# A mixture-of-experts layer whose first six batches are sorted by expert through a table in HBM, and the last two left dense

## The chip, the cores and the metric

The kernel runs on one core of one Trainium2 chip, as one launch. The metric is the device time of the launch in microseconds (us); before the change the median of three runs is 338.32 us (337.97 to 338.34). One core has five engines that run their own instruction streams in order and meet at semaphores: PE (matmuls; its weight loads are listed as PEld), DVE (vector), ACT (activations), POOL (GpSimd, which also issues the indirect DMAs) and SP, which only issues DMAs here.

## The reference, cut to what matters

```
h = embeddings[x]                              # 8 batches of 256 tokens, width 256
h = h + attention(layernorm(h))                # 16 heads of 16, rotary q and k, softmax
n = layernorm(h)
chosen = argmax(n @ gate_w.T)                  # one of 8 experts for each token
h = h + n + (n @ expert_w[chosen].T)
```

Everything is fp32. The kernel multiplies with float32r operands that are split into a high and a low part, so each product is three matmuls for each of the two halves of the contraction: high by high, low by high, high by low.

## The kernel before, in words

The kernel is a software pipeline over the eight batches, each of two tiles of 128 tokens (`NT = 2`). `steps` runs a step `b` from -3 to 9; each step has 16 slots, and in each slot every engine's program holds the pieces whose table entry falls on it. In step `b` stand, side by side: the attention of batch `b` (`visit`, eight visits in the even slots: scores of batch `b+1` for the row maxima, and transposed scores of batch `b` for `exp`; `outputs` in slots 5, 9, 13 and 1 of the next step), the front of batches `b+2` and `b+3` (layernorm, q/k/v projection, rotary sum on POOL, transposes; tables `FRONT` and `EARLY`), the part after attention of batch `b` or `b-1` (`POST`, and `LAST` for batch 7: output projection, residual, layernorm, gate, `choose`), and the experts of batch `b-2`. The step of the last attention is step 7; steps 8 and 9 hold what is left of batches 6 and 7.

`restack` (SP, L284 and L279) copies the split q and k of batch `b+2` into `stacks`, ten DMAs of 128 or 256 KB, and it starts when DVE has written the last low part (`qk_low`, front slot 4, slot 2 for the first four batches). `maximum` (SP, L269) brings the row maxima into the same buffer. `stacks` has three buffers.

The experts are dense: all 8 experts are computed for all tokens. `experts` on PE is called eight times for a batch, and each such unit is one token tile by two experts, 6 matmuls of 128x512 (`product`, L419). `select` on DVE (L881, L885) adds each expert's 128x256 result times a 0/1 mask. `finish` on POOL (L363) adds the two accumulators into `res`, and SP stores it (`store`, L289). `unit_in` says in which slots the units lie. The units of batches 0 to 4 share one PSUM bank, those of 5 to 7 use four.

Of the kernel before, what the change touches and what calls it, by code (L numbers as in the profile page):

```python
# [15 lines left out]
P = 128  # L16
# [5 lines left out]
VALS = 3  # L22


def rope_tables(n, hd):
# [7 lines left out]
    return np.ascontiguousarray(both.reshape(n // P, P, 2, hd).transpose(1, 0, 2, 3))  # L33


def tower(nc, x, emb, w_qkv, w_proj, gate_w, expert_w, rope, ramp, out):
# [12 lines left out]
    with ExitStack() as ctx:  # L49
# [11 lines left out]
        ramp_sb = sb("ramp_sb", [P, N_EXP])  # L61
# [20 lines left out]
        x_l = sb("x_l", [P, C, NT, P], F32R)  # L82
        rope_a = sb("rope_a", [P, NT, 2 * NH, HD])
# [9 lines left out]
        vals = [sb(f"vals{i}", [P, NT, NH, STRIP]) for i in range(VALS)]  # L93
        neg_max = sb("neg_max", [P, 2, NT, 8])
# [17 lines left out]
        yn = sb("yn", [P, NT, D])  # L112
        y_h = [sb(f"y_h{i}", [P, C, NT, P], F32R) for i in range(2)]
        y_l = [sb(f"y_l{i}", [P, C, NT, P], F32R) for i in range(2)]
        base = sb("base", [P, NT, D])
# [6 lines left out]
        res = sb("res", [P, NT, D])  # L122
# [37 lines left out]
        exp_ps, acc_ok, res_ok, out_ok = map(sem, "expert_ps acc_ok res_ok out_ok".split())  # L160

# [64 lines left out]
        def expert_banks(b):  # L226
# [23 lines left out]
        def _(sp):  # L250
# [5 lines left out]
            sp.dma_start(ramp_sb[:, :], ramp).then_inc(rope_in, 16)  # L256
# [29 lines left out]

            def store(b):
                wait(sp, res_ok, b + 2)
                sp.dma_start(out[b].rearrange("(t p) d -> p t d", p=P), res[:, :, :]).then_inc(out_ok, 16)  # L289

            def step(b, p):
# [9 lines left out]
                if here(b, -2):  # L301
# [12 lines left out]
            sp.wait_ge(out_ok, 16 * (NB + 1))  # L314
# [3 lines left out]
        def _(pool):  # L318
# [6 lines left out]
                            pattern=[[-1, P]], channel_multiplier=1).then_inc(ident_ok, 1)  # L325
            pool.wait_ge(ids_in, 16)

# [28 lines left out]
            def residuals(b):  # L356
                wait(pool, g_normed, b * NT + NT)
                g.tensor_tensor(base[:, :, :], h1[:, :, :], yn[:, :, :], ALU.add).then_inc(base_ok, 1)

            def finish(b):  # L360
                wait(pool, acc_ok, b * 16 + 17)
                wait(pool, out_ok, b * 16 + 16)
# [14 lines left out]
            def step(b, p):  # L377
                for s in range(SLOTS):
# [10 lines left out]
                    if s == 0 and here(b, -3):  # L389
                        finish(b - 3)  # L390
                    if s == 6 and b == -2:
# [18 lines left out]
        def _(pe):  # L410
# [156 lines left out]
            def y_transpose(b):  # L567
                wait(pe, g_normed, b * NT + NT)
                for c in range(C):
                    for t in range(NT):  # L570
                        k = (c * NT + t) * P
                        m = tr(m_bank[:, k:k + P], yn[:, t, c * P:(c + 1) * P], ident[:, :])
# [19 lines left out]
            def experts(b, p, n, banks):  # L592

# [395 lines left out]
```

## Time and the profile before

| | us |
|---|---|
| median of three runs | 338.32 (337.97 to 338.34) |
| the profiled execution | 337.72 |
| its span (first to last instruction) | 335.9 |
| PE busy / DVE busy / ACT busy / POOL busy | 280.2 / 244.5 / 118.4 / 84.7 |
| 16 DMA engines, share of the span on SP's queue | 38.6% |

The span is what the profile's rows lie in; the profiled execution's own time is 1.8 us longer, and it is 0.6 us under the median. PE's busy time is modelled, since matmuls overlap: a unit of six matmuls shows six records of about 0.40 us that start 0.23 us apart, so the pitch and not the length is the cost. PEclk is the granted TensorE clock, 1.00 for 2.4 GHz and 0.50 for 1.2 GHz.

### The profile page before, as it was taken

Reading aid. Unit: us, or ns where it says so; the run is one execution under the profiler, and the core shown is the slowest. Engines: PE = TensorE matmul, PEld = TensorE weight load, DVE = VectorE, ACT = ScalarE, POOL = GpSimd, SP = SyncE. Lnnn points to the kernel's source line nnn. Section 1 sums busy time; section 2 is a strip of 40 time slices with the busy share of each in tenths; the row PEclk is TensorE's granted clock in tenths of the full one; section 3 lists DMA queues with packets and bytes.
Section 4 is the critical chain, followed back from the end, with each engine's and each line's share of the span. In section 5 each row is a group of like instructions: output and inputs, shape, how many; then the busy total and the mean of one; then the engine's idle time right before and its main releaser. Section 6 shows DMA issues by size and latency. Waiting matters only on the chain.

```text
span 335.9 us, 5461 instructions
## 1 busy us (share of the span) xinstructions
PE 280.2 (83%) x2000; PEld 200.0 (60%) x2000; DVE 244.5 (73%) x595; ACT 118.4 (35%) x245; POOL 84.7 (25%) x96
## 2 busy tenths in 40 slices
PE   0457281877698899999999899989999999999894
PEld 0345170555465577766776677667766766667673
DVE  8353254678769887988798879887988885657763
ACT  3012131246354544434443444344434453441000
POOL 5235248472201310222032303220210121120211
PEclk9995755589979999999999999999999999999999
DMA  3619699009809608800790079008900000000000
GB/s 112 254 45 129 71 104 104 0 11 119 83 3 125 68 0 101 92 4 31 99 93 5 31 101 93 2 31 101 94 28 8 0 4 33 2 1 33 0 31 31
DMA packets 16197, 19.13 MB, mean 57 GB/s; under 512 B 2524, under 2 KB 13607, under 8 KB 16044
## 3 DMA queue, kind: packets, MB, share of 16 engines
q1 hardware_dynamic: 15404, 18.25, 38.6%
q0 software_dynamic: 768, 0.55, 1.3%
q8 instruction: 16, 0.26, 0.4%
q14 instruction: 9, 0.07, 0.1%
HBM read 5.30 MB, written 2.10 MB: 22 GB/s over the span
## 4 chain that ended last, share of the span: by engine, by line
PE 41%; DVE 23%; issue 11%; POOL 9%; DMA 7%; SPq 4%; ACT 3%; POOLq 0%; DVEq 0%; ACTq 0%
PE e_bank L419 13%; PE f_bank L419 7%; PE o_bank L536 6%; DVE acc L885 5%; DVE neg_max L806 4%; POOL qk L345 3%; PE t_pair L501 3%; DMA stacks<-parts 3%; DMA stacks<-max_rows 3%; SPq L284 3%; PE s_pair L419 2%; POOL h L332 2%; PE m_bank L548 2%; PE m_bank L419 2%; POOL res L363 1%
## 5 line engine op out<-in xcount | busy, mean ns | idle before, releaser
L687 ACT ACTIVATE probs<-t_pair 128x512 f32<-128x512 f32 x128 | 69.7, 597 | 91.4 <-PE t_pair L501 90.9
L806 DVE TENSOR_REDUCE neg_max<-s_pair 128x2 f32<-128x512 f32 x120 | 76.7, 681 | 14.0 <-PE s_pair L473 14.0
L419 PE MATMUL e_bank<-ew_h,y_h 128*128 128x512 f32 x92 | 40.4, 439 | 4.6 <-DVE acc L881 2.7
L501 PE MATMUL t_pair<-stacks 50*128 50x256 f32 x192 | 35.1, 310 | 3.9 <-DMA stacks<-max_rows 1.9
L885 DVE SCALAR_TENSOR_TENSOR acc<-e_bank,mask,acc 128x256 f32<-128x256 f32 x66 | 28.8, 477 | 11.3 <-PE e_bank L419 10.9
L501 PEld LDWEIGHTS t_pair<-stacks 50*128 50x128 f32 x192 | 24.4, 186 | 20.7 <-issue 17.1
L419 PE MATMUL e_bank<-ew_h,y_l 128*128 128x512 f32 x92 | 36.3, 395 | 0.0
L419 PE MATMUL e_bank<-ew_l,y_h 128*128 128x512 f32 x92 | 36.3, 395 | 0.0
L536 PE MATMUL o_bank<-probs,vals 128*32 128x256 f32 x512 | 35.1, 393 | 1.3 <-ACT max_rows L662 1.3
L473 PE MATMUL s_pair<-stacks 48*128 48x256 f32 x176 | 35.1, 325 | 0.4 <-DVE neg_max L806 0.4
L345 POOL TENSOR_TENSOR qk<-rope_a,rope_b 128x512 f32<-128x512 f32 x16 | 20.7, 1292 | 54.8 <-DVE rope_b L793 54.8
L419 PE MATMUL f_bank<-wqkv_h,x_h 128*128 128x256 f32 (+1 forms) x56 | 22.8, 407 | 10.8 <-DVE parts L798 6.5
L473 PEld LDWEIGHTS s_pair<-stacks 48*128 48x128 f32 x176 | 24.6, 197 | 1.5 <-DVE neg_max L806 0.6
L419 PEld LDWEIGHTS e_bank<-ew_h,y_h 128*128 128x128 f32 x92 | 17.3, 188 | 12.1 <-DVE acc L885 3.9
L429 PE MATMUL f_bank<-ident,xn 128*128 128x128 f32 x32 | 6.4, 333 | 19.5 <-DVE xn L774 18.8
L536 PEld LDWEIGHTS o_bank<-probs,vals 128*32 128x32 f32 x512 | 13.7, 110 | 14.1 <-issue 6.2
L419 PE MATMUL f_bank<-wqkv_l,x_h 128*128 128x256 f32 (+1 forms) x56 | 21.3, 380 | 0.0
L419 PE MATMUL f_bank<-wqkv_h,x_l 128*128 128x256 f32 (+1 forms) x56 | 21.2, 379 | 0.0
L419 PEld LDWEIGHTS f_bank<-wqkv_h,x_h 128*128 128x128 f32 x56 | 12.5, 222 | 14.2 <-DVE parts L798 7.3
L419 PEld LDWEIGHTS e_bank<-ew_l,y_h 128*128 128x128 f32 x92 | 17.3, 188 | 4.2
L352 POOL TENSOR_SCALAR g_ve<-g_mv 128x2 f32<-128x2 f32 x8 | 2.0, 252 | 69.8 <-DVE g_mv L765 69.8
L419 PEld LDWEIGHTS e_bank<-ew_h,y_l 128*128 128x128 f32 x92 | 17.4, 189 | 2.1
(123 smaller groups left out, 557.0 us busy)
## 6 DMA issues: line engine op xcount, KB each, us to landing
stacks<-parts SPq DMA_DIRECT2D x48, 128.0 KB
stacks<-parts SPq DMA_DIRECT2D x12, 256.0 KB
ew_raw<-in_expert_w SPq DMA_DIRECT2D x1, 2048.0 KB, 7.9
late_stacks<-parts SPq DMA_DIRECT2D x16, 128.0 KB
out<-res SPq DMA_DIRECT2D x8, 256.0 KB, 2.1
late_stacks<-parts SPq DMA_DIRECT2D x4, 256.0 KB
probs<-in_w_qkv SPq DMA_DIRECT2D x2, 384.0 KB, 3.4
stacks<-max_rows SPq DMA_DIRECT2D x24, 8.0 KB
```

Source lines behind the costliest of these rows:

```text
L284: sp.dma_start(stacks[b % STACKS][at:at + HD, :, k, :].bitcast(F32), parts[:, half, part, :].bitcast(F32)).then_inc(stack_in, 16)
L332: g.indirect_dma_start(h0[:, j, :], None, emb, bass.IndirectOffsetOnAxis(ap=ids[:, j:j + 1], axis=0), bounds_check=V - 1, oob_is_err=False ...
L345: g.tensor_tensor(qk[:, t, :, :, :].rearrange("p g d j -> p g j d"), rope_a[:, t, :, :].rearrange("p (g j) d -> p g j d", j=8), rope_b[:, ...
L419: m = mm(o, a(c), w(c), start=(n == 0), stop=(n == 3 * C - 1))
L429: m = tr(f_bank[:, k:k + P], xn[:, t, c * P:(c + 1) * P], ident[:, :])
L473: m = mm(score_pair(b, v)[:, half, t * N:(t + 1) * N], stacks[b % STACKS][r:r + KS, pair, 0, t * P:(t + 1) * P], stacks[b % STACKS][r:r + ...
L501: m = mm(t_pair[:, half, c * N:(c + 1) * N], stacks[b % STACKS][r:r + KM, pair, 1, c * P:(c + 1) * P], stacks[b % STACKS][r:r + KM, pair, ...
L536: m = mm(o_bank[STRIP * j:STRIP * (j + 1), 0:N], vals[b % VALS][:, c, head(4 * g + j), :], probs[:, (4 * g + j) % RING, c, :], start=(c == ...
L548: m = tr(strips_bank(b, t)[:, g * P:(g + 1) * P], o_t[:, g, t * P:(t + 1) * P], ident[:, :])
L687: nc.scalar.activation(probs[:, (2 * v + half) % RING, :, :].rearrange("p c n -> p (c n)"), t_pair[:, half, :], ACT.Exp, scale=SCALE).then ...
L806: v.tensor_reduce(neg_max[:, k // 4, :, 4 * half + k % 4], score_pair(b, k)[:, half, :].rearrange("p (t n) -> p t n", t=NT), AX.X, ALU.max ...
L885: v.scalar_tensor_tensor(out=acc[:, j, t, :], in0=y, scalar=mask[:, p, t, e:e + 1], in1=base[:, t, :] if u == 0 else acc[:, j, t, :], op0= ...
```

## The change

Batches 0 to 5 (`ROUTED = 6`) have no dense experts any more. For each of them PE counts with five small matmuls (`count_places`) how many tokens of each expert stand before each token, DVE turns that into a row number in a table in HBM (`find_rows`), in which each expert has its own region, and POOL scatters the layernormed rows with their residual base and their token number (2064 bytes for each token) into `sorted_rows` with two indirect DMAs (`send_rows`). This happens in slot 2 of step `b+2`. After batch 5, in step 7, DVE computes from the counts which expert and which first row each of 19 blocks of 128 rows has (`plan_blocks`, 17 small operations), and POOL writes 128 blank rows behind each expert's last one (`send_blanks`, 8 indirect DMAs). There are always 19 blocks, 12 + 7, whatever the tokens choose. They are taken in ten pairs (the last holds one block): SP fetches a pair (`fetch`, each block's row number read into a register), PE transposes it (`turn_blocks`), ACT and DVE split it (`block_top`, `block_rest`), PE multiplies each block by its one expert (`block_products`, 12 matmuls of 128x256 for a pair, the expert's column read into a register), DVE adds the base (`block_result`) and POOL scatters the rows to the output (`send_results`, an indirect DMA for each block). Pair `m` is turned in slot 11 + `m` counted from the start of step 7 and multiplied in the slot after. The buffers of fetched pairs are three. Batches 6 and 7 stay dense; batch 6's units move to slots 6 to 13 of step 8, behind the last pair, and batch 7's to the even slots of step 9, all with four banks.

`base` and `yn` get two buffers, with waits for the scatter two batches back. The small input `ramp` grows to a table of 284 columns. Two constant matrices are made on POOL at the start.

```diff
-            return [e_bank, f_bank] + s_bank if b >= NB - 3 else [e_bank]
+        expert_banks = [e_bank, f_bank] + s_bank
+        turn_bank = [f_bank, e_bank]
+        def place_at(b):
+            return SLOTS * (b + 2) + 2
+        def turn_at(m):
+            return SLOTS * (NB - 1) + 11 + m
...
-            slots = (0, 1, 2, 3, 5, 7, 8, 10) if b == NB else (1, 3, 5, 7, 9, 11, 13, 14) if b == NB - 1 else tuple(range(0, NH, 2))
+            slots = tuple(range(6, 14)) if b == NB else tuple(range(0, NH, 2))
...
+            def fetch(m):
+                if m == 0:
+                    sp.wait_ge(plan_ok, PLAN)
+                    sp.wait_ge(blanks_out, 16 * N_EXP)
+                    for i in range(2):
+                        sp.wait_ge(rows_out[i], 16 * NT * ROUTED // 2)
+                if m >= 3:
+                    sp.wait_ge(routed_out[(m - 3) % 2], sent(m - 3))
+                for j in blocks_of(m):
+                    row = sp.value_load(block_row[0:1, j:j + 1], min_val=0, max_val=N_EXP * REGION - P)
+                    sp.dma_start(fetched[m % 3][j % 2], sorted_rows[bass.ds(row, P), :]).then_inc(block_in[m % 3], 16)
...
+            def send_rows(b):
+                wait(pool, row_at_ok, b + 1)
+                wait(pool, row_ids_ok, b + 1)
+                wait(pool, base_ok, b + 1)
+                for t in range(NT):
+                    g.indirect_dma_start(sorted_rows, bass.IndirectOffsetOnAxis(ap=row_at[:, b, t:t + 1], axis=0),
+                                         rows[b % 2][:, t, :], None, bounds_check=N_EXP * REGION - 1,
+                                         oob_is_err=False).then_inc(rows_out[b % 2], 16)
+            def send_blanks():
+                g.memset(blank[:, 0:2 * D], 0.0).then_inc(blank_ok, 1)
...
+                for e in range(N_EXP):
+                    g.indirect_dma_start(sorted_rows, bass.IndirectOffsetOnAxis(ap=blank_at[:, e:e + 1], axis=0),
+                                         blank[:, :], None, bounds_check=N_EXP * REGION - 1,
+                                         oob_is_err=False).then_inc(blanks_out, 16)
+            def send_results(m):
+                wait(pool, block_ok, m + 1)
...
+                                         result[m % 2][:, j % 2, :], None, bounds_check=NB * N - 1,
...
-            def experts(b, p, n, banks):
+            def experts(b, p, n):
+                if k == 0 and n == 0:
+                    wait(pe, block_ok, PAIRS)
...
+            def count_places(b):
+                wait(pe, mask_ok, b * NT + NT)
+                mm(e_bank[:, 0:N_EXP], upper[:, :], mask[:, p, 0, :], start=True, stop=True)
...
+            def turn_blocks(m):
+                wait(pe, block_in[m % 3], fetches(m))
+                wait(pe, bl_ok, m - 1)
...
+                for j in blocks_of(m):
+                    for c in range(C):
+                        k = (j % 2 * C + c) * P
+                        i = tr(turn_bank[m % 2][:, k:k + P], fetched[m % 3][j % 2][:, c * P:(c + 1) * P], ident[:, :])
+                i.then_inc(bt_ps, 1)
+            def block_products(m):
...
+                wait(pe, bl_ok, m + 1)
+                wait(pe, block_ok, m - 1)
+                for j in blocks_of(m):
+                    w = pe.value_load(block_column[0:1, j:j + 1], min_val=0, max_val=(N_EXP - 1) * D)
+                    i = product(s_bank[m % 2][:, j % 2 * D:(j % 2 + 1) * D],
...
+                i.then_inc(block_ps, 1)
...
+                    for m in range(PAIRS):
+                        if g_at == turn_at(m):
+                            turn_blocks(m)
+                        if g_at == turn_at(m) + 1:
+                            block_products(m)
...
+            def block_top(m):
+                wait(act, bt_ps, m + 1)
...
+            def find_rows(b):
+                wait(dve, place_ps, b + 1)
...
+                            find_rows(k)
+                            if k == ROUTED - 1:
+                                plan_blocks()
```

## Rows read from the trace of the kernel before

**Rows 1.** The page's busy time by engine: busy us, share of the span, instructions.
```profile
PE 280.2 (83%) x2000; PEld 200.0 (60%) x2000; DVE 244.5 (73%) x595; ACT 118.4 (35%) x245; POOL 84.7 (25%) x96
```
**Rows 2.** Busy time by stretch, cut where an attention step begins; last three columns PEclk, DMA share, GB/s.
```profile
91.80:118.20 26.40, 23.13 (x202) 15.82 (x202) 21.83 (x55) 13.55 (x29) 5.56 (x7) 0.94 0.56 62
118.20:151.30 33.10, 32.29 (x252) 23.49 (x250) 27.96 (x69) 13.67 (x29) 5.83 (x7) 1.00 0.44 50
...
218.20:248.00 29.80, 28.66 (x235) 20.72 (x233) 23.96 (x55) 13.34 (x28) 4.73 (x5) 1.00 0.53 64
248.00:275.70 27.70, 26.77 (x216) 18.59 (x216) 23.36 (x59) 11.86 (x25) 3.50 (x4) 1.00 0.04 12
275.70:302.00 26.30, 26.06 (x187) 17.41 (x188) 15.09 (x48) 11.24 (x24) 3.90 (x5) 1.00 0.03 12
302.00:335.90 33.90, 27.58 (x142) 20.46 (x140) 20.82 (x60) 1.96 (x4) 5.63 (x6) 0.99 0.07 24
```
**Rows 3.** The chain that ended last, single pieces: start us, us, what.
```profile
42.48 2.94 PE f_bank L419 x12
...
59.77 1.10 PE f_bank L429 x4
...
195.59 1.44 PE f_bank L419 x12
...
299.20 1.40 PE s_pair L419 x6
...
302.42 1.00 PE o_bank L536 x16
303.42 1.60 PE f_bank L419 x6
...
306.42 0.44 PE m_bank L548 x4
...
314.51 0.07 issue
```
**Rows 4.** Groups of instructions over the whole run: count, busy us, mean ns, idle before.
```profile
L885 DVE SCALAR_TENSOR_TENSOR acc<-e_bank,mask,acc 128x256 f32<-128x256 f32 x66 | 28.8, 477 | 11.3 <-PE e_bank L419 10.9
...
L851 DVE TENSOR_TENSOR y_l<-m_bank,y_h 128x512 fp32r<-128x512 f32 x8 | 5.4, 679 | 1.2 <-ACT y_h L662 1.2
L662 ACT ACTIVATE y_h<-m_bank 128x512 fp32r<-128x512 f32 x8 | 4.7, 590 | 7.0 <-PE m_bank L572 6.9
...
L859 DVE TENSOR_REDUCE score<-m_bank 128x16 f32<-128x32 f32 x8 | 1.5, 182 | 1.3 <-PE m_bank L588 1.3
...
L321 POOL MEMSET ident<- 128x128 f32 x1 | 0.2, 205 | 0.4 <-POOLq L982 0.4
```
**Rows 5.** Timeline of SP's queue in the first step without experts: start us, us.
```profile
99.89 0.59 SPq L279 DMA_DIRECT2D stacks<-parts  x1
...
107.46 19.33 SPq L269 DMA_DIRECT2D late_stacks<-max_rows  x4
```
**Rows 6.** One microsecond at that restack's end, columns as in rows 2.
```profile
114.00:115.00 1.00, 1.00 (x20) 0.59 (x12) 0.90 (x2) 0.00 (x0) 0.02 (x1) 1.00 0.33 35
```
**Rows 7.** Timeline of POOL: the second gather of batch 0.
```profile
4.91 1.00 POOL L332 DMA_INDIRECT h<-in_emb,ids  x1 [0.30 <-DVE h L949]
```
**Rows 8.** Timeline of DVE: its first instruction that reads that gather.
```profile
7.38 0.42 DVE L762 BATCH_NORM_STATS2 f_st<-h 128x6 f32<-128x256 f32 x1
```
**Rows 9.** DMA issues of the run: size, median us from issue to landing.
```profile
out<-res SPq DMA_DIRECT2D x8, 256.0 KB, 2.1
...
probs<-in_w_proj SPq DMA_DIRECT2D x1, 256.0 KB, 2.8
```
**Rows 10.** Tile `h`, all 16 gathers: from issue to landing.
```profile
DMA to landing us min/median/max: 5.2/7.8/10.9
```
**Rows 11.** Two stretches of four microseconds, columns as in rows 2.
```profile
62.00:66.00 4.00, 3.73 (x11) 2.56 (x12) 2.18 (x5) 1.04 (x3) 2.52 (x2) 0.55 0.00 0
66.00:70.00 4.00, 2.89 (x18) 1.88 (x17) 3.96 (x7) 1.46 (x3) 2.30 (x2) 1.00 0.00 0
```

More of the change, by code:

```diff
@@ L82, in tower, with over @@
         x_l = sb("x_l", [P, C, NT, P], F32R)
+        ROW = 2 * D + 4
+        with ExitStack() as late:
+            def over(name, shape, dt=F32):
+                return late.enter_context(nc.sbuf_tensor(name, shape, dt))
+            blank = over("blank", [P, ROW])
+            blank_at = over("blank_at", [P, N_EXP], U32)
+            n_rows = over("n_rows", [P, N_EXP])
+            fuller = over("fuller", [P, N_EXP, ROUTED * NT])
+            n_blocks = over("n_blocks", [P, N_EXP])
+            lower = over("lower", [P, N_EXP, N_EXP])
+            block_end = over("block_end", [P, N_EXP])
+            block_start = over("block_start", [P, N_EXP])
+            begun = over("begun", [P, BLOCKS, N_EXP])
+            ended = over("ended", [P, BLOCKS, N_EXP])
+            owner = over("owner", [P, BLOCKS, N_EXP])
+            shift = over("shift", [P, N_EXP])
+            first_row = over("first_row", [P, BLOCKS, N_EXP])
+            owned_row = over("owned_row", [P, BLOCKS, N_EXP])
+            row_sum = over("row_sum", [P, BLOCKS])
+            column_sum = over("column_sum", [P, BLOCKS])
+            block_row = over("block_row", [P, BLOCKS], I32)
+            owned_column = over("owned_column", [P, BLOCKS, N_EXP])
+            block_column = over("block_column", [P, BLOCKS], I32)
+            result = [over(f"result{i}", [P, 2, D]) for i in range(2)]
+            res = over("res", [P, NT, D])
         rope_a = sb("rope_a", [P, NT, 2 * NH, HD])
@@ L300, in step @@
                     maximum(b + 1, 0)
-                if here(b, -2):
+                if b == NB - 1:
+                    for m in range(PAIRS):
+                        fetch(m)
+                if here(b, -2) and not routed(b - 2):
                     store(b - 2)
@@ L325, in _, with upper_triangle @@
                             pattern=[[-1, P]], channel_multiplier=1).then_inc(ident_ok, 1)
+            g.memset(upper[:, :], 1.0).then_inc(pool_filled, 1)
+            g.memset(every[:, :], 1.0).then_inc(every_ok, 1)
             pool.wait_ge(ids_in, 16)
+            def upper_triangle():
+                pool.wait_ge(pool_filled, 3)
+                g.affine_select(out=upper[:, :], in_=upper[:, :], compare_op=ALU.is_ge, fill=0.0, base=0,
+                                pattern=[[1, P]], channel_multiplier=-1).then_inc(upper_ok, 1)
@@ L642, in step @@
                         outputs(b, (s - 5) // 4)
-                    if here(b, -2) and unit_in(b, s) is not None:
-                        experts(b - 2, p, unit_in(b, s), expert_banks(b - 2))
+                    for k in range(ROUTED):
+                        if g_at == place_at(k):
+                            count_places(k)
+                    for m in range(PAIRS):
+                        if g_at == turn_at(m):
+                            turn_blocks(m)
+                        if g_at == turn_at(m) + 1:
+                            block_products(m)
+                    if here(b, -2) and not routed(b - 2) and unit_in(b, s) is not None:
+                        experts(b - 2, p, unit_in(b, s))
                     for k in batches(post, "o0", g_at):
@@ new lines, in block_rest, with block_result @@
+            def block_rest(m):
+                n = len(blocks_of(m)) * D
+                wait(dve, bh_ok, m + 1)
+                wait(dve, block_ps, m - 1)
+                v.tensor_tensor(block_low[m % 2][:, 0:n], turn_bank[m % 2][:, 0:n], block_high[m % 2][:, 0:n].bitcast(F32),
+                                ALU.subtract).then_inc(bl_ok, 1)
+            def block_result(m):
+                n = len(blocks_of(m))
+                wait(dve, block_ps, m + 1)
+                if m >= 2:
+                    wait(dve, routed_out[m % 2], sent(m - 2))
+                both = wide_raw[:, 2 * (m % 3) * ROW:2 * (m % 3 + 1) * ROW].rearrange("p (j r) -> p j r", j=2)
+                v.tensor_tensor(result[m % 2][:, 0:n, :], s_bank[m % 2][:, 0:n * D].rearrange("p (j d) -> p j d", d=D),
+                                both[:, 0:n, D:2 * D], ALU.add).then_inc(block_ok, 1)
```

218 lines of the change are left out of this document (189 added, 29 removed).

## The prediction

> **What bounds the kernel now.** I read the busy times by engine first [rows 1]: PE is at 83%, DVE at 73%, but these are averages. So next the stretches, cut where an attention step begins [rows 2]. The reader is to see three regimes. The stretch from 91.8 has no experts yet and lasts 26.4 us. The three from 118.2 to 218.2 have a batch of dense experts each and last 100.0 us together, with PE busy 32.3 of 33.1: PE bounds them. From 218.2 the fronts run out (29.8, 27.7, 26.3), PE still full. The last 33.9 us are experts of batches 6 and 7 and the end. Then the chain that ended last [rows 3] gives what pieces of PE cost at each clock, and SP's and POOL's timelines and the DMA rows [rows 5 to 10] what the transfers cost.
>
> **What goes away.** A dense unit costs PE 1.40 us in the chain [rows 3], a batch of eight 11.2 us. DVE loses 16 selects of 0.477 us, 7.6 us [rows 4].
>
> **Steps 2 to 4 (118.2 to 218.2).** The floor by PE is 33.3 - 11.2 = 22.1 us. But the stretch from 91.8 is nearly what such a step becomes: the same attention, front and gate work, no experts, 26.4 us, PEclk 0.94 [rows 2]. Its slow clock at the start costs about 1.5 us; against that the new step adds five small matmuls (0.5), five small DVE operations of about 0.18 us plus hops (1.2, [rows 4]), and on POOL two scatters, which there nothing waits for. That makes 25 to 26. The other limit is the restack. In that stretch SP issued it at 99.89, 8.1 us in [rows 5], and the DMA engines were busy until about 115 [rows 6], so 15 us, and the scores that open the next step wait for it. The later fronts hand over two slots later, about as late as 8 to 9 us in, which gives 23.5 to 24.5 us, and the scatter of 528 KB lands on the same engines just then, up to 2 us more. I take 25.8 us for each step, because both limits end there; bounds 24 (no interference) and 28 (the scatter adds whole, the clock falls). Three steps: 77.4 instead of 100.0.
>
> **Step 5 (29.8).** PE's part would be 18.6, but batch 7's restack still runs: 24.5, bounds 23 and 27. **Step 6 (27.7).** No restack left; PE 16.5, DVE 23.4 - 7.6 + 1.2 = 17.0: with their waits on one another 19, bounds 17.5 and 21. Saved so far: 22.6 + 5.3 + 8.7 = 36.6 us, and step 7 begins at 239.1 instead of 275.7 (bounds 231 and 250). Everything ahead of 118.2 stays: the larger table is loaded in the shade of the first projections, the constants are made while POOL waits for the ids.
>
> **Until the first block is there.** This is where the change pays. Counting from step 7's start, on one path: counts on PE in slot 2, 3.5 us; find the rows, 1.2; row numbers and two scatters on POOL, 2.9, since an indirect DMA takes POOL 1.00 us and 0.30 between [rows 7]; the blank tile's memset, four times the 0.205 us one, with a hop 0.9 [rows 4]; eight blank DMAs, 8 x 1.3 = 10.4; landing of the last, 2.1 as a store [rows 9]. That is 21.0, with nothing that could shorten it, since POOL is in order and the plan on DVE (17 small operations, some 6 us) is done before. Then SP loads a row number, issues (0.6, [rows 5]), loads the next, issues, and the second lands after 2.8 [rows 9]. Nothing in the trace shows a register load. Its bounds are 0.2 us (the 0.18 us small operation, [rows 4]) and 2.1 (a whole store, [rows 9]); I take 0.6, SP's time for one issue. The fetch is 4.6, so PE has its first pair 25.6 us into step 7 (bounds 20 and 30; indirect DMAs in a busy queue landed only after 5.2 to 10.9, [rows 10], while gather two of batch 0 was used 2.5 us after its issue, [rows 7, 8]). In the old kernel the whole step took 26.3 [rows 2]; here the slots up to 10 take less than the 25.6, and PE, ACT and DVE, all in order, stand at slot 11 with attention visits 6 and 7 behind them. POOL's rsqrt for batch 6's layernorm sits behind the blanks as well, but is there at 20.
>
> The Trainium skill, page "DMA: Bandwidth & Descriptors", section "Latency and other measured facts", puts the floor of a register load at about 600 ns. By it the fetch would be the 4.6 us above; no row here shows it.
>
> **The ten pairs.** PE's program has products of pair m-1, then the turn of pair m, then products of pair m, so nothing of pair m's split overlaps with PE work. At 2.4 GHz: four transposes 0.5 (0.44 in [rows 3]), ACT 0.6, DVE 0.7 [rows 4], products 1.44 with fill 1.6 [rows 3], four hops 0.3 (each up to 0.07, [rows 3]), one exposed register load 0.6: 4.3 us. At 1.2 GHz the transposes are 1.1 and the products 2.9 [rows 3]: 6.2 us. A second loop is the ring of three buffers: from the turn to the products' end 4.3, result 0.7, two scatters until landed 1.3 + 2.5 [rows 7, 8], fetch 4.6, in all 13.4 for three pairs, 4.5 each (with the scatter landing after 5.2, 5.4 each). Which clock? PE would be busy 2 us of 4.5, with gaps of over 2. [...] I expect it to change back and forth and take 5.4 a pair, midway. Nine and a half pairs: 51.3. The slots also hold other PE and ACT work which now lies on this path: two visits (0.9), two `exp` pairs (2.2), two outputs of 1.0, batch 6's transposes and gate (1.4), batch 7's attention transposes (1.5): 8 us [rows 3, 4]. Together 59.3, bounds 45 and 75.
>
> **Behind the pairs.** Batch 6's first dense unit waits for all ten results. From 303.42, behind the last outputs, the old kernel ran 15 units and batch 7's remaining chain and ended at 335.9, 32.5 us [rows 3]. New: 16 units (+1.4), without the transposes now inside the pairs (-1.4), 1 us until the clock is up: 33.5, bounds 32 and 35.
>
> **Sum.** After step 7's start the old kernel took 335.9 - 275.7 = 60.2 us; the new one 25.6 + 59.3 + 33.5 = 118.4. So -36.6 + 58.2 = +21.6 us. On the profiled execution's 337.7 that is 359.3, on the median of 338.3 it is 359.9. I predict 360.
>
> **The rivals.**
> (a) *The pairs overlap* (ends faster). If the engines run ahead of each other so that a pair costs PE's work and one latency, 0.44 + 1.44 + 0.9, about 2.8 us, the block part is 9.5 x 2.8 + 8 = 34.6, the time 335. It decides below about 3.1 us a pair, at which the sum is even with 338.3. For it: PE is only 0.44 + 1.44 busy for a pair, and there are three buffers. Against: the order of PE's program above, and the 4.5 us ring.
> (b) *TensorE's clock stays at 2.4 GHz through the pairs.* It did at 66 to 70 with PE busy 72% [rows 11], and attention work fills some gaps. Then a pair is the ring's 4.5 us, the block part 50.8, and no waking up: 360 - 8.5 - 1 = 350.
> (c) *The loop doesn't shorten as far.* If the scatter and the restack add up, steps 2 to 5 are 28, 28, 28 and 27: 9 us more, 369. For it: the stretch from 91.8 has its DMA quiet only 3 us before the next step. Against: the scatter's 528 KB are a third of a restack's 1.5 MB.
> (d) *TensorE stays at 1.2 GHz through the pairs*: 6.2 us a pair, 9.5 x 0.8 = 7.6 more, 368. For it: the gaps of over 2 us in each pair, and the release at 62 to 66 only after a nearly full stretch [rows 11]. Against: the row after it.
> The Trainium skill, page "TensorE: Matmul & The Clock Gate", part 1, says that a throttled array is the default and activity releases it. By it sparse pairs would stay slow, 368 in place of 360; the rows at 62 to 70 show a release but not how sparse is too sparse.
> (e) *Indirect DMAs land late*, 5.2 us and more as most gathers did [rows 10], with the slow clock: about 7 us a pair, the start 28: 15 + 2 more, 377. Against: those gathers shared the engines with restacks.
>
> **How the numbers follow.** The forecast (350 to 371 for its own bounds) 0.40; (a) 0.17; (b) 0.17; (c) 0.10; (d) 0.10; (e) 0.06. A difference of 0.2%, 0.7 us, is about what a measurement of this kernel can tell. Only (a) ends faster; a small part of it falls within 0.2%: faster 0.15, same 0.02, slower 0.83. From 338 to 382 lie all but most of (a) and the tail of (e), under 2 in 10.
>
> **What would show it.** Steps 2 to 4 near 25.8 us with PE waiting at their start for a DMA; step 7 beginning near 239; POOL with eight indirect DMAs at a pitch of 1.3 us and a hole of over 8 us on PE before the first pair; then ten pairs at 4.5 to 6 us each with PEclk between 0.5 and 1; the first dense unit of batch 6 near 324 and 33 us to the end. The forecast is wrong in sign if the pairs come closer than 3.1 us, and in size if POOL's indirect DMA of 2 KB rows takes much else than 1.3 us, or a register load on PE or SP costs over 1 us: each 0.1 us on PE's path is 1 us in the end.

## The result: 366.5 us against 338.3

The changed kernel takes 366.52 us (365.30 to 367.32) where the kernel before took 338.33: 1.0815 times as long, interval 1.0777 to 1.0853. (A median is that of all executions and a ratio with its interval that of the fast ones, so the quotient of the two medians, here 1.083, can differ a little from the ratio.) The prediction was 360. It is slower as forecast; what follows is about which terms of the sum carried that, and where the other 6.5 us come from.

The busy times of the changed kernel, first part of its page, answer to [rows 1]:

```profile
PE 262.0 (72%) x1924; PEld 185.8 (51%) x1924; DVE 225.1 (62%) x567; ACT 124.3 (34%) x255; POOL 118.9 (33%) x140
```

Every busy time except ACT's and POOL's fell (PE by 18 us, DVE by 19), and the kernel got 28 us longer. So the work became less and the waiting more. The stretches, cut where a step begins, answer to [rows 2]:

```profile
94.60:121.30 26.70, 22.05 (x205) 15.06 (x204) 23.50 (x58) 13.44 (x29) 5.79 (x7) 1.00 0.55 62
...
148.80:176.20 27.40, 23.09 (x213) 16.07 (x212) 22.77 (x61) 13.71 (x29) 8.09 (x10) 1.00 0.46 79
...
203.70:227.30 23.60, 19.33 (x199) 13.55 (x198) 18.39 (x41) 13.37 (x28) 5.99 (x8) 1.00 0.60 91
227.30:250.40 23.10, 19.33 (x176) 12.79 (x176) 17.21 (x48) 11.90 (x25) 4.49 (x6) 0.85 0.07 26
250.40:276.30 25.90, 14.25 (x111) 9.29 (x110) 10.21 (x47) 8.10 (x17) 12.63 (x15) 0.74 0.37 129
276.30:331.70 55.40, 37.75 (x227) 30.14 (x228) 16.55 (x35) 9.69 (x19) 17.63 (x19) 0.78 0.37 108
331.70:364.90 33.20, 24.25 (x108) 18.50 (x106) 17.54 (x50) 0.97 (x2) 5.71 (x6) 0.95 0.05 17
```

Read them against the forecast. The loop's steps 2 to 4 are 27.45 us each, where 33.3 stood and 25.8 was predicted. Step 6 is 23.1 where 19 was predicted. Then come the last three rows, which are the change's own cost: 25.9 us until the first sorted rows are transposed (25.6 predicted), 55.4 for the ten pairs with all that lies among them (59.3), and 33.2 behind them (33.5). In the pair row PE is busy 38 of 55 us at a mean granted clock of 0.78.

How the first of these comes about, on POOL's timeline of step 7: two scatters of rows, then eight of blanks at a pitch of 1.28 us.

```profile
255.53 1.10 POOL L453 DMA_INDIRECT sorted_rows<-rows,row_at  x1 [7.61 <-DVE row_at L1108]
...
257.88 0.56 POOL L458 MEMSET blank<- 128x512 f32 x1
...
259.30 0.97 POOL L463 DMA_INDIRECT sorted_rows<-blank,blank_at  x1 [0.80 <-POOL blank L459]
...
268.23 0.97 POOL L463 DMA_INDIRECT sorted_rows<-blank,blank_at  x1 [0.30 <-issue]
```

PE meanwhile, its waits on the timeline: 4.5 us for `o_n`, which stands behind the plan on DVE, and 6.0 us for the first fetch.

```profile
259.45 1.12 PE L708 MATMUL m_bank<-ident,o_t 128*128 128x128 f32 x4 [4.52 <-DVE o_n L1043]
...
276.28 1.12 PE L791 MATMUL f_bank<-ident,ew_raw 128*128 128x128 f32 x4 [5.99 <-DMA ew_raw<-sorted_rows]
```

And one pair, all engines. PE's transposes, ACT's high part, DVE's low part, then PE again; the bracket on the last row is PE idle for 2.15 us, put down to DVE. DVE was done at 301.09, though, and the products started at 301.89.

```profile
298.68 1.05 PE L791 MATMUL f_bank<-ident,ew_raw 128*128 128x128 f32 x4
...
299.77 0.60 ACT L873 ACTIVATE stacks<-f_bank 128x512 fp32r<-128x512 f32 x1 [5.49 <-PE f_bank L791]
300.40 0.69 DVE L1160 TENSOR_TENSOR stacks<-f_bank,stacks 128x512 fp32r<-128x512 f32 x1 [0.79 <-ACT stacks L873]
...
301.89 0.58 PE L579 MATMUL s_pair<-ew_h,stacks 128*128 x1 [2.15 <-DVE stacks L1160]
```

### The profile page after: what moved, and what is told of

Same layout as the page of the kernel before. It is cut to its first block, busy times and chain, and to the rows that moved or that the text cites. A ratio compares the mean times of both kernels' runs of the same rounds, so it can differ in the third digit from the quotient of the medians.

```text
span 364.9 us, 5648 instructions
## 1 busy us (share of the span) xinstructions
PE 262.0 (72%) x1924; PEld 185.8 (51%) x1924; DVE 225.1 (62%) x567; ACT 124.3 (34%) x255; POOL 118.9 (33%) x140
## 3 DMA queue, kind: packets, MB, share of 16 engines
q1 hardware_dynamic: 16508, 21.83, 36.9%
## 4 chain that ended last, share of the span: by engine, by line
PE 42%; DVE 18%; issue 11%; ACT 9%; DMA 8%; POOL 7%; SPq 2%; POOLq 0%; ACTq 0%
PE f_bank L579 10%; PE o_bank L696 7%; PE s_pair L579 6%; PE t_pair L661 6%; ACT probs L898 4%; DVE neg_max L1026 4%; DMA stacks<-parts 3%; DMA ew_raw<-sorted_rows 2%; PE e_bank L579 2%; POOL h L479 2%; PE m_bank L732 2%; PE m_bank L708 1%; DVE xn L994 1%; POOL sorted_rows L463 1%; DVE rope_a L1009 1%
## 5 line engine op out<-in xcount | busy, mean ns | idle before, releaser
L661 PE MATMUL t_pair<-stacks 50*128 50x256 f32 x192 | 39.5, 329 | 5.1 <-DVE neg_max L1026 3.2
L633 PE MATMUL s_pair<-stacks 48*128 48x256 f32 x176 | 38.8, 339 | 0.7 <-DVE neg_max L1026 0.4
L470 POOL DMA_INDIRECT out<-result,ew_raw x19 | 18.6, 977 | 38.4 <-DVE result L1170 35.4
L579 PE MATMUL s_pair<-ew_h,stacks 128*128 x76 | 19.3, 349 | 16.0 <-DVE stacks L1160 12.1
L1170 DVE TENSOR_TENSOR result<-s_pair,ew_raw 128x512 f32<-128x512 f32 (+1 forms) x10 | 6.7, 665 | 29.5 <-PE s_pair L579 29.5
L579 PEld LDWEIGHTS s_pair<-ew_h,stacks 128*128 128x128 f32 x76 | 14.2, 231 | 20.8 <-issue 20.8
L453 POOL DMA_INDIRECT sorted_rows<-rows,row_at x12 | 12.4, 1037 | 32.8 <-DVE row_at L1108 31.0
L479 POOL DMA_INDIRECT h<-in_emb,ids x16 | 17.0, 1060 | 5.9 <-issue 4.0
L873 ACT ACTIVATE o_t<-o_bank 128x256 f32<-128x256 f32 x32 | 12.5, 391 | 9.8 <-PE o_bank L696 9.8
L589 PEld LDWEIGHTS f_bank<-ident,xn 128*128 128x128 f32 x32 | 4.5, 178 | 20.8 <-issue 19.8
```

Of the source, the lines that this page charges most:

```text
L453: g.indirect_dma_start(sorted_rows, bass.IndirectOffsetOnAxis(ap=row_at[:, b, t:t + 1], axis=0), rows[b % 2][:, t, :], None, bounds_check= ...
L470: g.indirect_dma_start(out.rearrange("b n d -> (b n) d"), bass.IndirectOffsetOnAxis(ap=fetched[m % 3][j % 2][:, 2 * D:2 * D + 1].bitcast(U ...
L479: g.indirect_dma_start(h0[:, j, :], None, emb, bass.IndirectOffsetOnAxis(ap=ids[:, j:j + 1], axis=0), bounds_check=V - 1, oob_is_err=False ...
L579: m = mm(o, a(c), w(c), start=(n == 0), stop=(n == 3 * C - 1))
L589: m = tr(f_bank[:, k:k + P], xn[:, t, c * P:(c + 1) * P], ident[:, :])
L633: m = mm(score_pair(b, v)[:, half, t * N:(t + 1) * N], stacks[b % STACKS][r:r + KS, pair, 0, t * P:(t + 1) * P], stacks[b % STACKS][r:r + ...
```

## The experiments

Twelve kernels. The first two leave work out, and the one with constants in place of register loads leaves out the choice of the block's expert; the others do the whole computation. A pitch is the time from the first pair's transposes to the last's, over nine.

### The loop: what makes a step 27.5 us long

**No routing at all.** `count_places`, `find_rows`, the plan, all scatters, blanks, fetches and pairs out; only attention and the dense batches stay. The calls are drawn together here; each stands on a line of its own.

```
-                            count_places(k)
-                            find_rows(k)
-                            number_rows(k); send_rows(k); send_blanks(); plan_blocks()
-                        turn_blocks(m), block_products(m), block_top(m), block_rest(m), block_result(m), send_results(m)
```

> Leaves out everything of the routing: no counts, no row numbers, no scatters, no blanks, no pairs. Batches 6 and 7 stay dense, and the outputs of batches 0 to 5 are never written. What stays is the attention loop and the dense tail. Theory H (the loop's steps are set by hand-offs between TensorE, VectorE and ScalarE, and the five small matmuls with their two waits are on that chain): steps 2 to 4 fall from 27.5 to 25.8-26.4 us, the 25.8 of the prediction. Rival D (transfers set the step: the restacks, pushed later by the scatters): 24 to 25 us, as both the scatters and the count go. Rival R (the step does not care about any of it): 27.5 stays. Whole kernel by H: 366.5 less 55 for the pairs, 6 for blanks and plan, 7 for the steps: about 298; by D about 292; by R about 305.

**The counts alone** are put back: `count_places` and `find_rows`, nothing behind them.

> As the run without routing, but with the five small matmuls and the five VectorE operations that find the rows of each batch; no row is sent, and nothing behind that is done. H: steps 2 to 4 are back at 27.2-27.5 us, since only the instructions on TensorE and VectorE are on the chain; 5 to 8 us above the run without routing. D: within 0.3 us a step of the run without routing, as the scatters are what is missing in both. The start is told apart too: step 1 began 2.6 us late in the changed kernel; if the run without routing still shows 94.6 against 92.0, the memsets, the larger table or the schedule of the start hold it, and not the routing.

Measured: 305.67 us without routing (0.9045 of the kernel before, 0.9013 to 0.9078), 311.88 with the counts (0.9228, 0.9164 to 0.9293). Stretches without routing, three steps of the loop and step 6:

```profile
119.00:146.70 27.70, 23.50 (x203) 16.06 (x203) 22.17 (x56) 13.61 (x29) 5.81 (x7) 0.94 0.53 59
146.70:173.10 26.40, 22.17 (x203) 15.01 (x202) 22.04 (x56) 13.49 (x29) 5.79 (x7) 1.00 0.56 62
...
224.60:243.50 18.90, 15.40 (x168) 10.13 (x166) 16.47 (x43) 11.85 (x25) 2.21 (x3) 1.00 0.01 3
```

With the counts alone, a step of the loop and step 6:

```profile
145.60:173.00 27.40, 23.09 (x213) 16.08 (x212) 22.75 (x61) 13.70 (x29) 5.80 (x7) 1.00 0.53 59
...
224.70:248.70 24.00, 20.70 (x176) 14.08 (x176) 16.64 (x44) 11.80 (x25) 2.21 (x3) 0.79 0.01 2
```

Three things follow. The scatters cost the loop nothing: with and without them a step is 27.45 us, to a hundredth. So D falls. The counts cost 1.05 us at the full granted clock (27.45 against 26.41). And the floor is 26.4, not 25: two of the three steps without routing took 27.8 with the mean clock at 0.94, so the run came out near the 305 of rival R and not at the 298 of H, although its one step at full clock was where H put it. For the same reason the three steps together lost only 0.3 us with the counts out (82.0 us against 82.3). The 6 us between the two runs, which H had expected from the loop, came from step 6 for the most part: 18.9 us without the counts, 24.0 with them. The longest waits of PE in a step are the same in both kernels; first the changed one (148.8 to 176.2), then the one without routing (146.7 to 173.1). Columns: total, times, longest.

```profile
PE o_bank L643 <- ACT o_t L873: 1.2, 1, 1.2
PE m_bank L748 <- ACT gate_rows L873: 0.9, 1, 0.9
PE f_bank L621 <- DVE rope_b L1013: 0.7, 1, 0.7
PE m_bank L579 <- DVE o_l L1049: 0.7, 1, 0.7
```

```profile
PE o_bank L634 <- ACT o_t L863: 1.2, 1, 1.2
PE m_bank L739 <- ACT gate_rows L863: 0.9, 1, 0.9
PE f_bank L612 <- DVE rope_b L1002: 0.7, 1, 0.7
PE m_bank L570 <- DVE o_l L1038: 0.7, 1, 0.7
```

Waits for ACT and DVE, none for a DMA: the step is hand-offs.

**Late fronts on two banks**, to take one of these hand-offs away.

```
         def early(k):
-            return k < 4
+            return True
```
with `count_places` waiting until the front has left `e_bank`, and the front's next use of it until the row numbers are out.

> The whole computation. The late fronts (batches 4 to 7) use the second bank and the earlier slots that the fronts of batches 0 to 3 use; the place counts take that bank after the front has left it. Theory F (the prediction took the step without experts as the floor of steps 2 to 4, but that step has an early front with two banks; with one bank the late front's hand-offs make the step 26.4 at full clock): steps 2 to 4 fall from 27.46 to 26.0-26.5, the counts' 1.05 staying; 3 to 5 us of gain, 362-363. Rival G (the front is not what holds the step): 27.4, or longer where counts and front meet on the bank, 366-369.

Measured 377.05 us (1.1101, 1.1029 to 1.1173): slower by 10, which is beyond both theories. The wait for `rope_b` went, and two others came on the same step. Its row follows the waits, and then a step of the same place with the fronts as they were, from the kernel with five buffers and the turn ahead (below), whose clock fell for a while:

```profile
PE e_bank L622 <- POOL qk L492: 1.3, 1, 1.3
PE o_bank L644 <- ACT o_t L874: 1.2, 1, 1.2
PE e_bank L774 <- DVE parts L1019: 0.7, 1, 0.7
```

```profile
148.58:179.44 30.86, 26.79 (x214) 19.00 (x212) 23.52 (x62) 13.67 (x29) 8.08 (x10) 0.83 0.50 70
```

```profile
118.95:147.72 28.77, 24.45 (x213) 17.19 (x212) 22.88 (x61) 13.82 (x29) 8.11 (x10) 0.94 0.52 75
```

This step is 30.9 us at a mean granted clock of 0.83: PE's busy time rose by 3.6 us for the same work, as it ran part of it at 1.2 GHz. The steps beside it took 28.7 us at 0.94 and 29.8 at 0.89. At 0.94 the two ways to place the fronts are thus level, 28.7 and 28.8, and what the edit lost is in the clock. Theory F is refuted in this form, and of G it holds that this front doesn't set the step; no step of this run had the full clock throughout. Which of the four hand-offs would shorten the step if it went stays open. The second row shows one thing more: with the same program a step is 27.45 us at the full clock and 28.8 at 0.94.

### The way to the first pair

**Four of the eight blanks from SyncE**, as plain transfers to a row number that it loads; the blank tile is filled half a step earlier.

```
+                    for e in range(N_EXP // 2, N_EXP):
+                        row = sp.value_load(blank_at[0:1, e:e + 1].bitcast(I32), ...)
+                        sp.dma_start(sorted_rows[bass.ds(row, P), :], blank[:, :]).then_inc(blanks_out_sp, 16)
```

> The whole computation. Four of the eight blocks of blank rows are written by SyncE with plain transfers from a row number it reads, four stay on GpSimd, and the blank tile is filled half a step earlier. Theory: the eight GpSimd scatters (1.28 us each) are on the path to the first fetch, so the first transposes of sorted rows come 5 to 6.5 us earlier (from 25.8 us into the step to 19.5-21) and the kernel takes 360.5-362 us. Rival: TensorE's own queue (the attention of batch 7) or the landing of the row scatters holds the first fetch: 1 us or less, 365.5.

Measured 362.20 us (1.0690, 1.0632 to 1.0747), 4.3 less. POOL, then SP, then PE on its timelines:

```profile
261.80 0.97 POOL L471 DMA_INDIRECT sorted_rows<-blank,blank_at  x1 [0.30 <-issue]
...
258.14 4.30 SPq L384 DMA_DIRECT2D sorted_rows<-blank  x4
268.23 3.68 SPq L394 DMA_DIRECT2D ew_raw<-sorted_rows  x4
...
272.31 0.90 PE L801 MATMUL f_bank<-ident,ew_raw 128*128 128x128 f32 x3 [2.27 <-DMA ew_raw<-sorted_rows]
```

The blanks' issues ended at 262.8, 13.5 us into the step instead of 18.8, as expected. But SP's first load of a row number began at 267.5, 4.7 us later, where it had come 2.0 us behind the last blank before: with blanks from two queues side by side the last ones landed later. The first turn stands 23.0 us into the step instead of 25.8, half of the 5 to 6.5 us that were expected. From issue to landing POOL's four blanks took 4.0 to 5.7 us and SP's four 2.6 to 5.1.

**The plan later, nothing else.** DVE's 17 plan operations move from slot 2 to slots 6 and 8 of step 7.

```
-                                plan_blocks()
+                                plan_blocks(0)      # the blanks' rows only
+                    if g_at in (place_at(ROUTED - 1) + 4, place_at(ROUTED - 1) + 6):
+                        plan_blocks((g_at - place_at(ROUTED - 1)) // 2 - 1)
```

> The whole computation: the changed kernel with nothing but the plan moved, as in the run before this one (VectorE's 17 plan operations behind the attention's normalisations of step 7). Theory P (in the changed kernel the first pair waits for the chain of counts, row scatters and eight blanks on GpSimd, and the 4.52 us wait for o_n lies beside it): within 1.5 us of the changed kernel, 365-367 us, the first turn still near 276; the same move that gave 6 us where the pairs stood later and the blanks were shared gives nothing here. Rival (the wait for o_n is on the path, or the clock it costs is): 4 us or more, 360-362.

Measured 365.43 us (1.0787, 1.0708 to 1.0865), not told apart from the changed kernel. PE's waits from step 7's start to the first turn show why:

```profile
PE f_bank L791 <- DMA ew_raw<-sorted_rows: 11.9, 1, 11.9
...
PE m_bank L708 <- DVE o_n L1043: 0.6, 1, 0.6
```

The wait for `o_n` fell from 4.5 to 0.6 us and the one for the first fetch rose from 6.0 to 11.9. The wait for `o_n` lay beside the path, as theory P has it.

### The pairs: serial path, or ring of three

**Turn ahead**: the turn of pair m+1 stands ahead of the products of pair m.

```
-                    for m in range(PAIRS):
+                    for m in reversed(range(PAIRS)):      # on TensorE and on VectorE
                         if g_at == turn_at(m):
                             turn_blocks(m)
                         if g_at == turn_at(m) + 1:
                             block_products(m)
```

> The whole computation. On TensorE the transposes of pair m+1 now stand ahead of the products of pair m, and on VectorE the low part of m+1 ahead of the result of m. Theory S (the pair's 5.6 us are a serial path through TensorE, ScalarE, VectorE and TensorE again, which nothing overlaps): the pitch falls to 4.3-4.7 us, the limit of the three fetch buffers, and the kernel to 356-358 us. Rival B (the ring of three buffers is already the limit, fetch to scatter): at most 2 us of gain, 364-366. Rival C (the half clock is the price of a sparse TensorE, and the pitch follows the clock): the pitch falls less, to 5.0, 361.

**Five pairs of fetch buffers** in the changed kernel's order (the two new ones where the qkv weights were).

```
-        block_in = [sem(f"block_in{i}") for i in range(3)]
+        block_in = [sem(f"block_in{i}") for i in range(5)]
+        fetched_pair += [w... [:, 0:2 * ROW].bitcast(F32) for w in (wqkv_h, wqkv_l)]
```

> The whole computation, order of the changed kernel, but five pairs of fetch buffers instead of three (the two new ones lie where the qkv weights were). In the run with the turn ahead the ring of three took 17.0 us from the turn of pair 0 to that of pair 3, and in the changed kernel 16.7. Theory S (the serial path through TensorE, ScalarE and VectorE sets the pitch of the changed kernel, the ring is only just behind it): pitch stays near 5.5 us, the single wait of 1.65 us at pair 7 goes, 364-366. Rival B (the ring sets the pitch): 4.7 us a pair, 357-359.

**Both.**

> The whole computation, the turn of pair m+1 ahead of the products of pair m, and five pairs of fetch buffers. Theory: the run with the turn ahead lost because with a ring of three the products stood in TensorE's queue behind a turn whose rows were not there. With five the turn is there in time and the split overlaps: 3.0-4.0 us a pair, set by SyncE's two fetches (2 x 1.3) and GpSimd's two scatters (2.55), so 342-350 us. Rival B2 (something else holds a pair, the half clock or ScalarE and VectorE between the attention work): 4.7-5.5 a pair, 357-366. Rival B3 (turning ahead is bad by itself): above 366.

| | median us | ratio to before, interval | pitch us |
|---|---|---|---|
| changed kernel | 366.52 | 1.0815, 1.0777 to 1.0853 | 5.68 |
| turn ahead | 375.96 | 1.1087, 1.1013 to 1.1161 | 6.51 |
| five buffers | 364.33 | 1.0770, 1.0712 to 1.0827 | 5.46 |
| both | 349.22 | 1.0330, 1.0282 to 1.0379 | 3.39 |

The turn ahead alone missed all three theories: it is slower. On its timeline, DVE has the low part of pair 2 at 285.2, so the products could follow; SP can fetch pair 3 only at 288.95, when the results of pair 0 have left; and in PE's order pair 3's turn is next:

```profile
285.23 0.69 DVE L1160 TENSOR_TENSOR stacks<-f_bank,stacks 128x512 fp32r<-128x512 f32 x1 [0.93 <-ACT stacks L873]
...
288.95 5.42 SPq L388 DMA_DIRECT2D ew_raw<-sorted_rows  x4
293.57 1.12 PE L791 MATMUL e_bank<-ident,ew_raw 128*128 128x128 f32 x4 [6.58 <-DMA ew_raw<-sorted_rows]
```

PE idles 6.6 us with pair 2's products behind the wait. Turn to turn, pairs 0 to 3, took 17.0 us (16.7 in the changed kernel). Five buffers alone give some 2 us, as theory S expects: the serial path set the pitch, the ring was right behind it. (The two intervals overlap; in the traces the one long gap, 7.6 us from pair 6's turn to pair 7's, became 5.5.) Only both together free the pairs: 3.4 us each, 17 us off the total. The two edits are worth -9, +2 and, together, +17.

**Constants in place of TensorE's register loads.**

```
-                    w = pe.value_load(block_column[0:1, j:j + 1], ...)
+                    w = (j * N_EXP // BLOCKS) * D
```

> As the changed kernel, but TensorE takes each block's expert from a constant instead of a register load, so the blocks are multiplied by the wrong expert's weights; the work on every engine is the same otherwise. The prediction priced the exposed load at 0.6 us a pair. Theory L (a load costs TensorE about 1.0 us from its start to the first matmul, once per block, and the second is partly covered by the first block's products): 1.2-1.6 us a pair less, 351-355. Rival L2 (the load runs while TensorE waits for the low part anyway): under 0.3 us a pair, 364-366.

Measured 362.41 us (1.0698, 1.0654 to 1.0742): 4.1 us less, 0.4 a pair, and the pitch on the trace is 5.16 instead of 5.68. That is between the two theories. But the reason that L2 gives, a load that runs while PE waits for the low part, is not what the traces show. In the program the load stands behind that wait. In the changed kernel DVE is done at 301.09 and PE starts at 301.89, and in all ten pairs that stretch is 0.78 us or more; with the constant it is 0.06 in nine and 0.15 in the first. One pair with the constant:

```profile
301.89 0.69 DVE L1160 TENSOR_TENSOR stacks<-f_bank,stacks 128x512 fp32r<-128x512 f32 x1 [0.66 <-ACT stacks L873]
...
302.64 0.50 PE L579 MATMUL s_pair<-ew_h,stacks 128*128 128x256 f32 x2 [1.41 <-DVE stacks L1160]
```

So the first load of a pair is exposed by 0.72 us, a little more than the 0.6 of the prediction. The pitch fell by less because the ring of three buffers then holds the pairs: behind the first one, PE waited 7.9 us for fetched rows here and 1.6 in the changed kernel.

### Together, and a version that beats both

**Together**: turn ahead, five buffers, blanks shared with SP, and batch 6's eight dense units between the pairs, in `t_bank` once the attention has left it.

> The whole computation: five pairs of fetch buffers, the turn ahead, four of the eight blanks from SyncE and the blank tile filled early, and batch 6's eight dense units between the pairs in the attention's two exponent banks (batch 7's second transpose goes to the output bank). If the gaps of the pair phase are real gaps, the 11 us of dense units fit into them and the clock stays up: 11 to 14 us below the run with ring and turn alone from this, 4 from the blanks, so 328-336 us, below the kernel before. Rival: the units delay the pairs by their own length, since TensorE would then be full (2.0 + 1.4 us of work in a pitch of 3.0-3.5): 338-345.

**Pairs four slots later**, `turn_at` from slot 11 to slot 15, batch 6's units following.

> The whole computation, the kernel of all changes together with the block pairs four slots later in the step, so that batch 7's last two attention visits stand ahead of the first pair (TensorE had 6.7 us idle before it) and batch 7's output, projection and layernorm chain runs between pairs 3 to 9. In the run with all together TensorE was busy 36.8 of 39 us in the pairs but waited 4.5 and 4.6 us once each behind them for that chain. Theory: 8 to 11 us of these holes go, 334-337 us, at or just below the kernel before. Rival: the chain's hand-offs now stop the pairs instead, since every engine runs in order, and the time stays at 343-346.

**And the plan later**, the edit shown above, on top.

> The whole computation: the kernel with the pairs later, and VectorE's 17 plan operations (4.2 us) moved from slot 2 of step 7 behind the attention's normalisations, in two halves at slots 6 and 8; only the blank rows' numbers stay at slot 2. In the run with the pairs later TensorE waited 4.59 us at 251.9 for o_n behind the plan, and its granted clock was 0.5 from 257.6 to about 283. Theory: the wait falls to about 1 us and the clock is at full speed for most of that stretch, where TensorE had 20 us of work; 6 to 10 us less, 330-334 us, faster than the kernel before by 1 to 2.5%. Rival: the stretch up to the first pair is bound by the rows' arrival (first turn not before 270) and the clock falls in another gap, 337-339 us.

| | median us | ratio to before, interval |
|---|---|---|
| together | 344.83 | 1.0215, 1.0136 to 1.0295 |
| pairs later | 339.62 | 1.0041, 1.0013 to 1.0070 |
| plan later too | 333.26 | 0.9817, 0.9788 to 0.9846 |

The run with all together, stretches from step 7's start, cut at the first turn and behind the last pair:

```profile
248.20:269.90 21.70, 15.82 (x111) 10.43 (x109) 9.54 (x45) 6.85 (x15) 6.49 (x8) 0.69 0.45 156
269.90:309.00 39.10, 36.90 (x256) 29.75 (x257) 22.23 (x49) 10.61 (x22) 18.82 (x20) 1.00 0.51 152
309.00:340.20 31.20, 18.09 (x77) 13.64 (x75) 12.86 (x38) 0.97 (x2) 6.12 (x7) 0.85 0.05 17
```

The middle row is what the change needs: PE busy 36.9 of 39.1 us at a granted clock of 1.00, ten pairs and eight dense units inside. It missed its 328 to 336: although batch 6's eight units are gone from the last row, it still takes 31.2 us with PE busy 18. There PE waits 4.5 us for batch 7's rows (`rows`, DVE), where the changed kernel waited 1.7 with dense units at hand; that the whole of the 31.2 comes from batch 7's own chain is argued from this, not shown. Moving the pairs behind the last attention visits shortened that row to 19.5 us, but a stretch ahead of them grew, and its 334 to 337 were missed by 3 us. The same three stretches with the pairs later, up to the first turn; and with the plan later, all three:

```profile
247.50:276.90 29.40, 21.27 (x144) 13.25 (x142) 10.98 (x48) 11.38 (x24) 8.17 (x9) 0.65 0.58 181
```

```profile
249.50:270.20 20.70, 16.67 (x143) 10.43 (x142) 11.02 (x48) 11.28 (x24) 8.19 (x9) 0.92 0.49 165
270.20:310.90 40.70, 37.83 (x245) 32.19 (x244) 24.82 (x59) 7.25 (x13) 18.80 (x20) 0.92 0.51 146
310.90:332.70 21.80, 13.88 (x54) 10.62 (x54) 9.76 (x27) 0.37 (x1) 4.74 (x5) 0.86 0.08 24
```

The plan on DVE made PE wait there for `o_n`:

```profile
256.60 1.11 PE L727 MATMUL m_bank<-ident,o_t 128*128 128x128 f32 x4 [4.59 <-DVE o_n L1068]
```

Behind that gap the outputs took 1.94 us instead of 1.07, the half clock, which held for most of the way up to the first pairs. With the plan moved the stretch is 8.7 us shorter: 4 us of wait, and PE's busy time for the same work 21.3 to 16.7 as the mean clock went from 0.65 to 0.92. The edit that gave nothing alone gives 6.4 us here, because here PE's work and not the first fetch sets that stretch. The result is 5.1 us below the kernel before, 1.5 to 2.1% by the interval.

## Why the prediction was nearly right, point by point

- **Ahead of step 2: unchanged.** In the profiled execution step 2 began at 121.3, 3.1 us late. In nine other kernels with the same program up to there it began between 118.2 and 120.4, as the 118.5 of before. So most of this is variation between executions, though 121.3 lies outside that range; the two latest, 121.3 and 120.4, are those whose step 0 had a mean granted clock of 0.80 and 0.79, where the others had 0.93.
- **Steps 2 to 4, 25.8 us each: 27.45.** This is the term that was mis-sized most, by 5.0 us in all. Its parts, added as they stand, already give more than it says: 26.4 - 1.5 + 0.5 + 1.2 is 26.6, not 25 to 26. The larger error is the step that it started from [rows 2]. Step 1 has an early front (batches 0 to 3: earlier slots, two banks), steps 2 to 4 have the later one. The 1.5 us taken off for the slow clock were right for step 1; in the kernel with everything together that step had the full clock throughout and took 24.9:

```profile
93.31:118.21 24.90, 21.83 (x202) 15.05 (x202) 21.91 (x55) 13.44 (x29) 5.46 (x7) 1.00 0.59 66
```

 A step with the later front and no counts takes 26.41 at the full clock, 1.5 us more. Its waits for `o_t` (1.2 us) and `rope_b` (0.7) are not among those of step 1; that they make the 1.5 us is not shown. (The changed kernel's own step 1 took 26.7 at the full clock. It followed the slow step 0 and had a wait of 1.6 us for POOL that the other one lacks.) The small operations, put at 1.7, cost 1.05, and 26.6 + 1.5 - 0.65 is the 27.45 measured. The second limit that the prediction named, restack plus scatter, is nothing: scatters out, same step, and the wait for a DMA at the step's start, named as its sign, is not there.
- **Step 5, 24.5: 23.6.** Held.
- **Step 6, 19: 23.1.** The second mis-sized term, by 4.1 us. Without routing this step is 18.9 at clock 1.00; with the counts alone 24.0 at 0.79; in the changed kernel 23.1 at 0.85. So the 19 were right for the work, and the counts and the slower clock that comes with them make the rest. The prediction had put no slow clock here. That the scatters don't is shown; why the clock falls in this step with the counts and not without them is not.
- **The first pair, 25.6 us into step 7: 25.8.** Its pieces hold too: 5.1 until the first row scatter (4.7 predicted), 3.8 until the first blank (3.8), 9.9 for eight (10.4), 2.0 of landing (2.1), 5.1 for the fetch (4.6). The fetch's loads were the unknown. From the start of a load to the issue it is 1.0 us the first time and 0.7 later; SP's queue in the trace has the load itself at

```profile
L387 SPq TENSOR_LOAD <-block_row x19: 262/268/493, 271.2 to 321.9; - x19
L387 SPq FUSED_REGOPS  x19: 152/152/187, 271.7 to 322.2; - x19
```

 The Trainium skill, page "DMA: Bandwidth & Descriptors", section "Latency and other measured facts", gives about 600 ns as the floor of a register load; these rows show less for the load and the operation behind it (268 + 152 ns, 0.42 us) and a little more from the load's start to the issue (0.7).
- **The pairs, 59.3: 55.4.** 5.68 us a pair with what lies among them, where the forecast has 59.3 / 9.5, 6.2 us; the clock changed back and forth (0.78 on average), as forecast. How the 0.5 us splits between the pair (5.4) and the 8 us among them is not shown. The exposed register load, put at 0.6 a pair, is 0.72. The ring of three was put at 13.4 us for three pairs and took 16.9 and 17.0 in the two kernels where PE waited for the fourth pair's rows (constants, turn ahead). The changed kernel didn't show this error, since its serial path took 16.7 for the same three.
- **Behind the pairs, 33.5: 33.2.** Held.
- **The sum.** Start +3.1, steps 2 to 4 +5.0, step 5 -0.9, step 6 +4.1, first pair +0.2, pairs -3.9, end -0.3: 7.3 us, and the span is 364.9 where 357.5 was forecast. The start and the loop erred by 11 us one way and the pairs by 4 the other, so that the total is as near as it is by some luck.
- **The rivals.** (a), overlapping pairs, did not happen, and the reason given (the order of PE's program, and the ring) is shown: it takes both edits to get there. Then a pair is 3.4 us with what lies among them, close to what (a) has (34.6 / 9.5, 3.6 us); its price was right, its condition was not met. (That run's 349 us stand above (a)'s 335 mainly because step 7 began at 249.4 and not at 239.1.) (b) and (d), one clock throughout, are out: 0.78 on average, both levels in turn. (c), scatter and restack adding up, named the right place with the wrong cause: the loop was longer than forecast, but by the later front's step, the sum's own slip and, in step 6, counts and clock. (e), late landings, is out here: 2.0 us behind the blanks; it showed only where two queues wrote at once.

## What to carry to other kernels

A shorter PE program shortens a step only down to its hand-offs: read the floor off a step of the same kind, with the same waits, at the same clock. Here the kind made 1.5 us (24.9 against 26.4 at the full clock) and a spell at half clock 1.3 to 1.4 (28.8 against 27.45, 27.8 against 26.4). In a software pipeline over in-order engines, count the buffers before you turn the order round: a load issued ahead with its buffer still taken puts ready work behind a wait. And a hole that is worth nothing on one schedule can be worth its length and the clock on the next; try the edit again when the path has moved.

## What was not expected of the hardware

- A gap can cost twice. PE's busy time for one and the same stretch of work was 21.3 us after a wait of 4.6 us (mean granted clock 0.65) and 16.7 without that wait (0.92).
- Four plain transfers of 258 KB beside four indirect ones of the same size: the last had landed 4.7 us behind the last issue, where eight indirect ones in one queue landed 2.0 us behind theirs. Halving the queue's 10 us gained 2.8 us.
- An indirect DMA of 128 rows takes POOL 0.97 us (1.1 for the first of a group) and 0.30 to the next, for rows of 1 KB (results) and of 2 KB (rows and blanks) alike.
- A register load on PE that stands behind a wait is not covered by it: 0.78 us from DVE's end to the first matmul with the load, 0.06 without.
